# Softmax's causal zeroes written by GpSimd, with the units and the maxima in another order

## The chip, the cores and the metric

One Trainium2 chip, one of its cores. The metric is the device time of one launch in microseconds. Times of this kernel are the median of several launches; the profile is of one launch of its own.

## The reference, cut to what matters

The program is two transformer-like layers on x of 4 batches x 512 tokens x 128 features; each has a half-weighted feed-forward, attention, and another half-weighted feed-forward (first layer: dense; second: eight experts). The change touches the first layer's softmax attention alone, 16 heads of width 8:

```python
q, k, v = (_heads(q), _heads(k), _heads(x))
scores = jnp.einsum('bhqd,bhkd->bhqk', q, k) * scale
causal = jnp.tril(jnp.ones((t, t), dtype=bool))
scores = jnp.where(causal, scores, -jnp.inf)
y_ar = jnp.einsum('bhqk,bhkd->bhqd', jax.nn.softmax(scores, axis=-1), v)
e = v[:, :, 1:, :] - y_ar[:, :, :-1, :]
...
ma = jnp.einsum('bhqd,bhkd->bhqk', qa, ka)
ma = jnp.where(jnp.tril(jnp.ones((t - 1, t - 1), dtype=bool)), ma, 0.0)
y_ma = jnp.einsum('bhqk,bhkd->bhqd', ma, e)
```

So the softmax's answers y_ar are needed before the second, linear part (y_ma) of the same attention.

## The kernel before, in words

Each engine runs its own program, written out by hand: `nc.tensor` (PE), `nc.vector` (DVE), `nc.scalar` (ACT), `nc.gpsimd` (GpSimd, POOL in the profile) and `nc.sync` (SP, which issues the loads). They meet only in semaphores, and each engine's instructions, DMA issues included, run in the order of its program. `hold` (L310) is a wait that its engine makes before going on.

**Stages, sets, units, steps.** Attention of the first layer runs once for each batch b, as stage 0 to 3. In a stage the 16 heads are taken in four sets of four heads (hs, set 0 to 3). The 512 queries and 512 keys are cut in four tiles each; with causal masking 10 of the 16 pairs (key tile kt, query tile qt) remain. A pair for one set is one product of 128 keys x (4 heads x 128 queries), 512 columns. Five units i of two pairs each (`EXP_PAIRS`, L106, taken two by two) make a set, so a stage has 20 units, NX; a turn of the PE loop over u = 5 hs + i (L1636) is called a step here, step 0 to 4 of its set.

**Two passes.** The softmax subtracts a true row maximum. First pass, for batch b+1 while batch b is in its second: `max_scores` (L1541) makes a pair's scores with queries on partitions into one of two PSUM banks (`max_banks`), adds -1e30 above the diagonal by a second matmul (identity times `add_q_bf`), and DVE's `maxima` (L1100) reduces it to 128x4; 10 pairs a set, two in each step, the next on a bank only when its reduction is done. `max_of_tiles` and `max_turn` finish it, ACT writes the maxima as `mT`, and SP's `max_row` (L396) puts them as an extra row into the operand of the second pass. Stage 3 has no next batch and no first pass beside it.

Second pass: `scores` (L1561) makes unit u+2 in step u, into `pair[u % 2]`, as soon as the exponential of unit u has been read out of it. On a diagonal pair (kt = qt) a second matmul adds -1e30 to the forbidden places (`ident_bf` times `add_k_bf`, bf16, L1573). ACT's `attention` (L839) exponentiates both pairs of a unit at once, 128x1024 (L846), into the ten slots of `banks` (`sb_work` in the profile), which the next set overwrites; so it waits for the values products of the set before that read them (`LAST_OF_UNIT`). `answers` (L1576) multiplies a key tile's exponentials, all queries from the diagonal on (512, 384, 256 or 128 columns for kt 0 to 3), by the values, 4 heads in `accum[0]`, summed over kt. It runs in the step in which the last exponential of that tile is due: kt 0 in step 1, kt 1 in step 3, kt 2 and 3 in step 4. After a set ACT copies the sum out (`answers_out`, L832; it stands behind unit 0 of the next set), PE turns it in step 1 of the next set (`turn_answers`, L1588), DVE divides (`answers_divide`, L1139), and GpSimd makes the errors v - y (`errors`, L641). DVE's order of reductions and divisions is written in `at` (L1156), with the moments and the normalisation of batch b-1 (`moments`, `normalise`) between them; GpSimd supplies their inverse deviations (`rsqrt`) and later the bias (`add_bias`).

**SP.** In a stage before the last, SP goes set by set (L460): it holds until all ten maxima of the set are made (`smax_mm`), loads the maximum set two further (5 DMAs), holds for the scores of the set (`st_mm`), and loads the exponential set two further (5 DMAs) with its row of maxima (1 DMA). In stage 3 it holds for `st_mm` alone. Ahead of the sets stand `load_state` (the features of the linear part, 2 MB) and `load_values`. `scores` waits for `xset` at the first unit of a set (L1565).

```python
# SP, L460
for hs in range(NS):
    if b + 1 < B:
        next_max_set(b + 1, hs)
    hold(sp, s["st_mm"], NX * b + NG_X * (hs + 1))
    if hs + 2 < NS:
        load_exp_set(b, hs + 2)
        max_row(b, hs + 2)
```

After the four sets comes the linear part of the stage (`ma_scores`, `ma_answers`), which the change leaves as it is.

## Time and profile before

| | us |
|---|---|
| median of 3 runs | 645.68 (642.53 to 649.96) |
| the profiled execution, its own time | 643.67 |
| its span in the profile | 641.9 |
| PE busy | 521.5 (81%) |
| DVE busy | 359.4 (56%) |
| ACT busy | 197.0 (31%) |
| GpSimd busy | 189.0 (29%) |
| mean granted PE clock | 0.953 |

The span is from the first to the last instruction of the profiled execution. Busy time of an engine counts its instructions, not waits or the issue of DMAs. A matmul's end is modelled, and successive matmuls overlap: their pitch is the difference of their starts. The chain is the sequence of work that ended last, followed back from the end to whatever released each piece. All four attention stages together are the stretch from 115 to 343 us (115 to 173, 173 to 235, 235 to 296, 296 to 343).

### The profile page before, as it was taken

Reading aid. Unit: us, or ns where it says so; the run is one execution under the profiler, and the core shown is the slowest. Engines: PE = TensorE matmul, PEld = TensorE weight load, DVE = VectorE, ACT = ScalarE, POOL = GpSimd, SP = SyncE. Lnnn points to the kernel's source line nnn. Section 1 sums busy time; section 2 is a strip of 40 time slices with the busy share of each in tenths; the row PEclk is TensorE's granted clock in tenths of the full one; section 3 lists DMA queues with packets and bytes.
Section 4 is the critical chain, followed back from the end, with each engine's and each line's share of the span. In section 5 each row is a group of like instructions: output and inputs, shape, how many; then the busy total and the mean of one; then the engine's idle time right before and its main releaser. Section 6 shows DMA issues by size and latency. Waiting matters only on the chain.

```text
span 641.9 us, 10406 instructions
## 1 busy us (share of the span) xinstructions
PE 521.5 (81%) x3895; PEld 326.7 (51%) x3895; DVE 359.4 (56%) x942; ACT 197.0 (31%) x282; POOL 189.0 (29%) x228
## 2 busy tenths in 40 slices
PE   0788767999899989989877897894888878788893
PEld 0555333444544463445345773693345556663693
DVE  4753666466766767685044564132587888853131
ACT  0455331453154324424633450120223221110120
POOL 5676463010011102011110346654321212322163
PEclk9996798999999999999998997997998999988998
DMA  7317978732353244225269912323275455211320
GB/s 245 147 34 219 283 234 279 199 115 61 91 148 83 93 87 143 59 59 114 78 129 141 290 59 100 96 87 91 91 221 161 112 163 147 79 34 36 95 64 9
DMA packets 73666, 79.85 MB, mean 124 GB/s; under 512 B 10946, under 2 KB 50499, under 8 KB 73360
## 3 DMA queue, kind: packets, MB, share of 16 engines
q1 hardware_dynamic: 71056, 73.61, 41.4%
q0 software_dynamic: 2560, 5.58, 2.5%
q8 instruction: 31, 0.51, 0.3%
q14 instruction: 19, 0.16, 0.1%
HBM read 44.07 MB, written 35.72 MB: 124 GB/s over the span
## 4 chain that ended last, share of the span: by engine, by line
PE 49%; DVE 20%; issue 7%; DMA 6%; ACT 6%; POOL 5%; SPq 5%; POOLq 0%; DVEq 0%; ACTq 0%
PE ps_accum L1428 21%; PE ps_pair L1428 18%; PE ps_turn L1428 6%; DMA sb_ring<-sb_qs 3%; PE ps_turn L1436 2%; DVE sb_work L1178 2%; SPq L356 2%; POOL sb_rstd L569 2%; DVE sb_work L1323 2%; DVE sb_stats L1001 2%; DVE sb_mpart L1104 2%; SPq L350 1%; POOL xe_scr L589 1%; DMA sb_cols<-in_bias_cols 1%; PE ps_turn L1593 1%
## 5 line engine op out<-in xcount | busy, mean ns | idle before, releaser
L846 ACT ACTIVATE sb_work<-ps_pair 128x1024 f32<-128x1024 f32 x80 | 80.3, 1026 | 52.6 <-PE ps_pair L1428 51.8
L1104 DVE TENSOR_REDUCE sb_mpart<-ps_turn 128x4 f32<-128x512 f32 x80 | 55.0, 688 | 28.2 <-PE ps_turn L1428 28.1
L1428 PE MATMUL ps_pair<-sb_ring,sb_xsets 128*128 128x512 f32 x160 | 62.3, 465 | 6.7 <-ACT sb_work L846 3.5
L1104 DVE TENSOR_REDUCE sb_mpart<-ps_accum 128x4 f32<-128x512 f32 x80 | 55.0, 688 | 19.1 <-PE ps_accum L1428 18.3
L1428 PE MATMUL ps_pair<-sb_ident_bf,sb_ones_bf 128*128 128x512 bf16 x189 | 52.5, 437 | 12.1 <-DMA sb_x<-y_scr 7.8
L1428 PE MATMUL ps_accum<-sb_work,sb_v_aug 128*32 128x128 f32 (+3 forms) x768 | 53.9, 393 | 0.3 <-ACT sb_work L846 0.3
L1428 PE MATMUL ps_turn<-sb_ring,sb_m_sets 128*128 128x512 f32 x80 | 38.1, 477 | 9.4 <-DVE sb_mpart L1104 9.2
L567 POOL TENSOR_SCALAR sb_ve<-sb_mv 128x4 f32<-128x4 f32 x24 | 5.5, 228 | 133.5 <-DVE sb_mv L1004 126.9
L1428 PE MATMUL ps_accum<-sb_ring,sb_m_sets 128*128 128x512 f32 x80 | 40.6, 507 | 4.4 <-DVE sb_mpart L1104 3.8
L650 POOL TENSOR_TENSOR sb_e_pad<-sb_v_next,sb_y_ar 128x128 f32<-128x128 f32 x16 | 7.4, 460 | 122.8 <-DVE sb_y_ar L1148 122.8
L1428 PEld LDWEIGHTS ps_pair<-sb_ident_bf,sb_ones_bf 128*128 128x128 bf16 x189 | 20.4, 110 | 37.5 <-issue 13.2
L1323 DVE TENSOR_TENSOR sb_work<-ps_pair,sb_cst 128x1024 f32<-128x1024 f32 x32 | 37.5, 1214 | 2.2 <-PE ps_pair L1428 2.1
L1428 PEld LDWEIGHTS ps_pair<-sb_ring,sb_xsets 128*128 128x128 f32 x160 | 29.7, 192 | 17.7 <-issue 6.3
L1178 DVE TENSOR_TENSOR sb_work<-ps_pair,sb_cst 128x1024 f32<-128x1024 f32 x32 | 37.7, 1219 | 0.9
L1428 PE MATMUL ps_accum<-sb_mw,sb_work 128*128 128x128 f32 x256 | 31.3, 276 | 2.7 <-issue 2.7
L1272 DVE SCALAR_TENSOR_TENSOR sb_y_tmp<-ps_accum,sb_expert_rows 128x128 f32<-128x128 f32 x32 | 9.8, 347 | 42.0 <-PE ps_accum L1428 42.0
L1428 PE MATMUL ps_pair<-sb_y_tmp,sb_mw 128*128 128x256 f32 x128 | 30.7, 383 | 2.0 <-ACT sb_y_tmp L902 2.0
L1428 PE MATMUL ps_pair<-sb_xs,sb_w1r 128*128 128x512 f32 x64 | 23.6, 500 | 10.7 <-DVE sb_xs L1020 7.5
L589 POOL DMA_INDIRECT xe_scr<-sb_exit_rows,sb_slot_all x16 | 15.9, 995 | 53.4 <-DVE sb_slot_all L1085 49.8
L1428 PEld LDWEIGHTS ps_accum<-sb_mw,sb_work 128*128 128x128 f32 x256 | 30.0, 192 | 3.1 <-issue 3.0
L1428 PEld LDWEIGHTS ps_accum<-sb_work,sb_v_aug 128*32 128x32 f32 x768 | 18.8, 111 | 19.6 <-issue 13.4
L1428 PEld LDWEIGHTS ps_accum<-sb_ring,sb_m_sets 128*128 128x128 f32 x80 | 15.0, 188 | 25.9 <-DVE sb_mpart L1104 18.8
(251 smaller groups left out, 991.3 us busy)
## 6 DMA issues: line engine op xcount, KB each, us to landing
sb_expert_rows<-xe_scr SPq DMA_DIRECT2D x16, 258.0 KB, 2.8
sb_m_sets<-q_scr SPq DMA_DIRECT2D x16, 256.0 KB
sb_xsets<-k_scr SPq DMA_DIRECT2D x16, 256.0 KB
sb_ka_stk<-mk_scr SPq DMA_DIRECT2D x4, 1024.0 KB
xe_scr<-sb_cst SPq DMA_DIRECT2D x4, 1024.0 KB, 12.8
sb_mw<-in_mw SPq DMA_DIRECT2D x16, 256.0 KB, 6.1
sb_ka_stk<-mk_scr SPq DMA_DIRECT2D x8, 512.0 KB
q_scr<-sb_qs SPq DMA_DIRECT2D x12, 256.0 KB, 3.4
```

What stands on the lines that cost most here:

```text
L356: sp.dma_start(ring[VW * hl:VW * hl + 3 * HD, i, hl].bitcast(F32), head_rows(q_scr, b, HL * hs + hl, 3 * HD)).then_inc(done, 16)
L569: pool.tensor_tensor(rstd[i][:], ve[i][:], const("minus_half"), ALU.pow).then_inc(s["rstd"], 1)
L589: pool.indirect_dma_start(xe_scr[m], bass.IndirectOffsetOnAxis(ap=slot_all[:, i:i + 1], axis=0), rows_out[m][b][:, t, :], None).then_inc(s ...
L650: pool.tensor_tensor(dst, value, answer, ALU.subtract).then_inc(s["err_pad"], 1)
L846: act.activation(banks[:, 2 * i:2 * i + 2], pair[u % 2][:], ACT.Exp, scale=SCALE).then_inc(s["exp_done"], 1)
L1001: dve.bn_stats(stats[i][:, t, :], src[:, t, :]).then_inc(s["stats"], 1)
L1104: dve.tensor_reduce(mpart[:, m // NPAIR, m % NPAIR, :], max_banks[m % 2][:].rearrange("p (h k) -> p h k", h=HL), AX.X, ALU.max).then_inc(s ...
L1178: dve.tensor_tensor(work[:, n % 4].rearrange("p a (h q) -> p (a h) q", h=HL), pair[n % 2][:].rearrange("p a (h q) -> p (a h) q", h=HL), bc ...
L1272: last = dve.scalar_tensor_tensor(out=ye[n % 2][:, g, :], in0=accum[n % 2][:, g * D:(g + 1) * D], scalar=xg[:, n % 4, g, GATE:GATE + 1], i ...
L1323: dve.tensor_tensor(work[:, n % 4].rearrange("p a (h q) -> p (a h) q", h=HL), pair[n % 2][:].rearrange("p a (h q) -> p (a h) q", h=HL), bc ...
L1428: return pe.matmul(dst, lhsT, rhs, start=start, stop=stop, skip_group_check=True)
L1436: last = pe.transpose(tile(dst, t), src[:, t, 0:D], ident)
```

## The change

The mask matmul of the second pass goes: `scores` no longer adds -1e30 on diagonal pairs. The exponentials above the diagonal are written, whatever they are, and GpSimd then overwrites them with zero in place (`clear_late`, one `affine_select` for each unit that holds a diagonal). The units are regrouped (`EXP_UNITS`): (0,0) (0,1); (0,2) (0,3); (2,2) (3,3); (1,1) (2,3); (1,2) (1,3), so three selects a set, of 128x512, 128x1024 and 128x512. Values products run kt 0 in step 1, 3 in step 2, 2 in step 3, 1 in step 4, and each waits for GpSimd's `late_zero` as well. ACT copies the previous set's sum behind unit 1 instead of unit 0. The ten maxima of a set, two a step before, are spread 1, 3, 1, 2, 3 over its steps (`MAX_BESIDE`: before the values product, behind it, behind the turn), and DVE takes up nine of them before it normalises, not six. GpSimd's `rsqrt` and `add_bias` come behind the clears of set 0 and of unit 0 in set 1. The first pass keeps its mask matmuls, and SP's program is unchanged.

```diff
+EXP_UNITS = [((0, 0), (0, 1)), ((0, 2), (0, 3)), ((2, 2), (3, 3)), ((1, 1), (2, 3)), ((1, 2), (1, 3))]
+ANSWER_ORDER = [0, 2, 3, 1]
+READY_AT = [max(i for i, unit in enumerate(EXP_UNITS) for kt, qt in unit if kt == t) for t in range(NT)]
+LAST_OF_UNIT = [max(ANSWER_ORDER.index(kt) for kt, qt in unit) for unit in EXP_UNITS]
+CLEARED_UNITS = [i for i, unit in enumerate(EXP_UNITS) if any(kt == qt for kt, qt in unit)]
+MAX_BESIDE = [(1, 0, 0), (1, 1, 1), (1, 0, 0), (1, 0, 1), (1, 0, 2)]
...
+            def clear_late(b, hs, j):
+                i = CLEARED_UNITS[j]
+                pool.wait_ge(s["exp_done"], NX * b + NG_X * hs + i + 1)
+                weights = diagonal_slots(i).rearrange("p n (h q) -> p n h q", h=HL)
+                pool.affine_select(weights, weights, [[0, weights.shape[1]], [0, HL], [1, P]], ALU.is_ge, 0.0,
+                                   base=0, channel_multiplier=-1).then_inc(s["late_zero"], 1)
...
             def attention(b):
+                for j in range(len(CLEARED_UNITS)):
+                    clear_late(b, 0, j)
                 if b:
                     rsqrt(norm_first(B + b - 1), (b - 1) % 2)
-                    add_bias(norm_first(B + b - 1), b - 1, 0, s["ffn_base"])
-                for hs in range(NS - 1):
-                    errors(b, hs)
+                for hs in range(1, NS):
+                    clear_late(b, hs, 0)
+                    if b and hs == 1:
+                        add_bias(norm_first(B + b - 1), b - 1, 0, s["ffn_base"])
+                    clear_late(b, hs, 1)
+                    errors(b, hs - 1)
+                    clear_late(b, hs, 2)
...
-                    act.activation(banks[:, 2 * i:2 * i + 2], pair[u % 2][:], ACT.Exp, scale=SCALE).then_inc(s["exp_done"], 1)
-                    if hs and i == 0:
+                    act.activation(unit_slots(i), pair[u % 2][:], ACT.Exp, scale=SCALE).then_inc(s["exp_done"], 1)
+                    if hs and i == 1:
                         answers_out(b, hs - 1)
...
-                    at = [6] + [NPAIR * (hs + 1) + 3 for hs in range(NS - 1)] + [NM]
+                    at = [9] + [NPAIR * (hs + 1) + 3 for hs in range(NS - 1)] + [NM]
                     maxima(b + 1, 0, 4)
                     if b:
                         moments(norm_first(B + b - 1), x[b - 1], (b - 1) % 2)
-                    maxima(b + 1, 4, 6)
+                    maxima(b + 1, 4, 9)
...
-                    kt, qt = EXP_PAIRS[2 * i + a]
-                    last = mm(pair[u % 2][:, a, :], tile(x_sets[:, hs % 2], kt), ring[:, hs % 2, :, qt * P:(qt + 1) * P],
-                              stop=kt != qt)
-                    if kt == qt:
-                        last = mm(pair[u % 2][:, a, :], ident_bf[:], bc(add_k_bf[:], HL), start=False)
+                    kt, qt = EXP_UNITS[i][a]
+                    last = mm(pair[u % 2][:, a, :], tile(x_sets[:, hs % 2], kt), ring[:, hs % 2, :, qt * P:(qt + 1) * P])
...
-                pe.wait_ge(s["exp_done"], NX * b + NG_X * hs + (first + NT - kt - 1) // 2 + 1)
+                pe.wait_ge(s["exp_done"], NX * b + NG_X * hs + READY_AT[kt] + 1)
+                zeroed = next(j for j, i in enumerate(CLEARED_UNITS) if (kt, kt) in EXP_UNITS[i])
+                pe.wait_ge(s["late_zero"], len(CLEARED_UNITS) * (NS * b + hs) + zeroed + 1)
...
+                    m = NPAIR * hs + sum(map(sum, MAX_BESIDE[:i]))
+                    ends = [m + sum(MAX_BESIDE[i][:n]) for n in range(4)]
                     if ahead:
-                        max_scores(b + 1, 2 * u, 2 * u + 1)
-                    for kt in range(NT):
-                        if (DIAGONAL[kt] + NT - kt - 1) // 2 == i:
+                        max_scores(b + 1, ends[0], ends[1])
+                    for kt in ANSWER_ORDER:
+                        if READY_AT[kt] == i:
                             answers(b, hs, kt)
+                    if ahead:
+                        max_scores(b + 1, ends[1], ends[2])
                     if hs and i == 1:
                         turn_answers(b, hs - 1)
                     if ahead:
-                        max_scores(b + 1, 2 * u + 1, 2 * u + 2)
+                        max_scores(b + 1, ends[2], ends[3])
```

`slot_of`, `unit_slots` and `diagonal_slots` give the two slots of a unit, and those of its diagonals, in `banks`, whose layout is as before.

## Rows read from the trace of the kernel before

**Rows 1.** The page: chain by engine, and the exponential's group.
```profile
PE 49%; DVE 20%; issue 7%; DMA 6%; ACT 6%; POOL 5%; SPq 5%; POOLq 0%; DVEq 0%; ACTq 0%
...
L846 ACT ACTIVATE sb_work<-ps_pair 128x1024 f32<-128x1024 f32 x80 | 80.3, 1026 | 52.6 <-PE ps_pair L1428 51.8
```

**Rows 2.** Busy us by window, stages 1 and 3: PE, PEld, DVE, ACT, POOL, clock.
```profile
173.00:235.00 62.00, 56.57 (x432) 29.81 (x430) 42.72 (x77) 23.92 (x27) 6.63 (x12) 1.00 0.36 99
...
296.00:343.00 47.00, 40.53 (x371) 20.79 (x370) 15.88 (x33) 22.39 (x26) 6.04 (x11) 1.00 0.63 124
```

**Rows 3.** Chain in order of time: start us, us, what; stages 1 and 3.
```profile
192.51 2.67 DMA sb_ring<-sb_qs
...
197.62 0.46 PE ps_pair L1428 x2
...
199.76 0.69 PE ps_pair L1428 x3
...
307.66 3.17 DMA sb_ring<-sb_qs
```

**Rows 4.** SP's queue in order of time: start us, us; stages 0, 1, 3.
```profile
127.26 1.54 SPq L364 DMA_DIRECT2D sb_ring<-k_scr  x4
...
138.23 1.52 SPq L364 DMA_DIRECT2D sb_ring<-k_scr  x4
...
149.57 1.52 SPq L364 DMA_DIRECT2D sb_ring<-k_scr  x4
...
188.49 1.54 SPq L364 DMA_DIRECT2D sb_ring<-k_scr  x4
...
199.85 1.51 SPq L364 DMA_DIRECT2D sb_ring<-k_scr  x4
...
302.89 4.33 SPq L356 DMA_DIRECT2D sb_ring<-q_scr  x4
```

**Rows 5.** PE in order of time, stage 1: start us, us, [idle before].
```profile
186.44 0.50 PE L1428 MATMUL ps_turn<-sb_ring,sb_m_sets 128*128 128x512 f32 x1 [0.54 <-DVE sb_mpart L1104]
186.87 0.86 PE L1428 MATMUL ps_accum<-sb_work,sb_v_aug 128*32 128x256 f32 x16
187.66 0.50 PE L1428 MATMUL ps_accum<-sb_ring,sb_m_sets 128*128 128x512 f32 x1
...
190.99 1.07 PE L1428 MATMUL ps_accum<-sb_work,sb_v_aug 128*32 128x512 f32 x8
191.99 0.66 PE L1593 MATMUL ps_turn<-sb_cst,sb_y_tmp 128*128 128x128 f32 x4
192.40 0.48 PE L1428 MATMUL ps_accum<-sb_ring,sb_m_sets 128*128 128x512 f32 x1
...
194.05 0.51 PE L1428 MATMUL ps_accum<-sb_ring,sb_m_sets 128*128 128x512 f32 x1 [0.25 <-DVE sb_mpart L1104]
...
195.23 0.49 PE L1428 MATMUL ps_pair<-sb_ring,sb_xsets 128*128 128x512 f32 x1 [0.44 <-DMA sb_ring<-sb_qs]
```

**Rows 6.** PE in order of time, stage 3.
```profile
315.71 0.72 PE L1428 MATMUL ps_pair<-sb_ring,sb_xsets 128*128 128x512 f32 x2 [0.74 <-ACT sb_work L846]
...
323.50 0.72 PE L1428 MATMUL ps_pair<-sb_ring,sb_xsets 128*128 128x512 f32 x2 [0.74 <-ACT sb_work L846]
...
328.64 1.19 PE L1428 MATMUL ps_pair<-sb_qa_pad,sb_ka_stk 128*128 128x512 f32 x4
```

**Rows 7.** GpSimd's groups by line, 80 to 343 us: count, busy us, mean ns.
```profile
L650 POOL TENSOR_TENSOR sb_e_pad<-sb_v_next,sb_y_ar 128x128 f32<-128x128 f32 x16 | 7.4, 460 | 122.8 <-DVE sb_y_ar L1148 122.8
...
L691 POOL MEMSET sb_qa_pad<- 128x8192 f32 x1 | 6.9, 6929 | 0.0
L574 POOL TENSOR_TENSOR sb_x<-sb_x,sb_rows 128x512 f32<-128x512 f32 x4 | 5.1, 1272 | 3.7 <-DVE sb_kaf L1010 1.2 <-DVE sb_qf L1010 1.2 <-DVE sb_kf L1010 1.2
L569 POOL TENSOR_TENSOR sb_rstd<-sb_ve,sb_cst 128x4 f32<-128x4 f32 x3 | 3.1, 1037 | 0.3
...
L638 POOL COPY sb_v_aug<-sb_values 128x512 f32<-128x512 f32 x4 | 2.4, 610 | 21.1 <-DMA sb_values<-v_scr 11.1 <-PE ps_accum L1428 10.0
```

More of the change, by code:

```diff
@@ L96 @@
 ma_hi ma_lo mq_kept mk_kept state_in ka_t_mm ka_tok v_aug smax_mm smax_red max_t
-max_t_evac st_mm exp_done pv_mm y_evac y_t rcp y_norm err err_pad ma_mm ma_masked
+max_t_evac st_mm exp_done late_zero pv_mm y_evac y_t rcp y_norm err err_pad ma_mm ma_masked
 kv_mm kv_evac ym_mm yar_mm yar_evac y_sum proj_mm attn_base attn_x lg_mm lg_max lg_sub lg_exp
@@ L106 @@
 EXP_PAIRS = [(kt, qt) for kt in range(NT) for qt in range(kt, NT)]
-DIAGONAL = [EXP_PAIRS.index((t, t)) for t in range(NT)]
-LAST_OF_UNIT = [EXP_PAIRS[2 * i + 1][0] for i in range(NPAIR // 2)]
+EXP_UNITS = [((0, 0), (0, 1)), ((0, 2), (0, 3)), ((2, 2), (3, 3)), ((1, 1), (2, 3)), ((1, 2), (1, 3))]
[4 more added lines that the diff above has]
+MAX_BESIDE = [(1, 0, 0), (1, 1, 1), (1, 0, 0), (1, 0, 1), (1, 0, 2)]
 NM, NX, NG_X = NS * NPAIR, NS * NPAIR // 2, NPAIR // 2
@@ L121, in psum, with unit_slots, diagonal_slots @@
             return ctx.enter_context(nc.psum_tensor("ps_" + name, shape, F32))
+        slot_of = {pair: n for n, pair in enumerate(EXP_PAIRS)}
+        def unit_slots(i):
+            a, b = (slot_of[pair] for pair in EXP_UNITS[i])
+            return banks[:, a:b + 1:b - a]
+        def diagonal_slots(i):
+            a = [slot_of[pair] for pair in EXP_UNITS[i] if pair[0] == pair[1]]
+            return banks[:, a[0]:a[-1] + 1:max(a[-1] - a[0], 1)]
         s = {n: ctx.enter_context(nc.semaphore("s_" + n)) for n in SEMS}
@@ L1578, in answers @@
                 w = T - P * kt
-                first = EXP_PAIRS.index((kt, kt))
-                pe.wait_ge(s["exp_done"], NX * b + NG_X * hs + (first + NT - kt - 1) // 2 + 1)
+                first = slot_of[kt, kt]
+                pe.wait_ge(s["exp_done"], NX * b + NG_X * hs + READY_AT[kt] + 1)
+                zeroed = next(j for j, i in enumerate(CLEARED_UNITS) if (kt, kt) in EXP_UNITS[i])
+                pe.wait_ge(s["late_zero"], len(CLEARED_UNITS) * (NS * b + hs) + zeroed + 1)
                 if kt == 0 and hs >= 1:
@@ L1584, in answers @@
                     last = mm(accum[0][VW * hl:VW * hl + VW, kt * P:T], v_aug[:, kt, HL * hs + hl, :],
-                              banks[:, first:first + NT - kt, hl * P:(hl + 1) * P], start=kt == 0, stop=kt == NT - 1)
+                              banks[:, first:first + NT - kt, hl * P:(hl + 1) * P], start=kt == 0, stop=kt == ANSWER_ORDER[-1])
                 last.then_inc(s["pv_mm"], 1)
```

## The prediction

> **What bounds the kernel now.** I read the page's header and its chain by engine first [rows 1]: TensorE (PE) carries 49% of the chain that ended last, and SP's queue with the DMAs 11%. The table by stage [rows 2] has one row for each of the four attention stages, 228 us of the 641.9; stages 1 and 3 stand for them. In stage 1 (0 and 2 are alike), where PE also makes the next batch's maxima, PE is busy 56.57 of 62 us, 91%, at full granted clock, and GpSimd 6.63. Stage 3 has no maxima and PE is at 86%.
>
> Then the chain in order of time [rows 3]. In stage 1 it does not run along PE alone. The last maximum of set 0 ends about 188.4 and releases SP, which issues five loads of the next-but-one maximum set, five of the exponential set and one row of maxima [rows 4]. The row is issued at 192.51 and lands at 195.18, and only then does PE start set 2's first scores, in step 3 of set 1. PE waits 0.44 us there [rows 5]. So there is a loop: last maximum of a set, SP and DMA, steps 3 and 4 of the next set, its last maximum. It costs 195.23 - 188.4 = 6.8 plus 199.8 - 195.2 = 4.5, so 11.3 us; SP's own starts are 199.85 - 188.49 = 11.36 apart, in stage 0 10.97 and 11.34 [rows 4]. PE's work fits inside with a few tenths to spare. The loop holds sets 1 and 2 of stages 0 to 2, but not set 0 (its loads are in) nor set 3 (nothing is loaded for its steps 3 and 4).
>
> **The mask matmuls.** In the chain a group "x3" (two score products and a mask) takes 0.69 to 0.70 and "x2" 0.46 [rows 3], so a mask, like a product, is 0.23 us. The change drops 4 in a set, 64 in all: 14.7 us of PE work. What they are worth:
> Sets 1 and 2 of stages 0 to 2: steps 0 to 2 lose three masks (0.7), hand one maximum product and its mask to later steps (0.46), and take in key tile 3's values product (0.26, a third of the 0.79 from 186.87 to 187.66 [rows 5]). PE reaches step 3 about 0.9 us earlier and waits that much longer for the row. Steps 3 and 4 lose one mask, gain one maximum product and one of its masks (+0.23 net), and hold 640 instead of 768 columns of values products (-0.26): 4.5 us stays 4.5. SP's trigger stays the last maximum. Gain 0.
> Set 0: in stage 0 five masks lie on the path, 1.15 us; in stages 1 and 2 it starts at DVE's update of x, behind which lie four, 0.92. There PE also waits twice for reductions behind DVE's moments and normalisation, the second time 0.54 us [rows 5], together about one. The uneven spread leaves one maximum in step 2 beside the moments and moves the normalisation behind nine; I count 0.5 us of waits left, so 0.5 gained. Together 1.15 + 2 x 1.42 = 4.0.
> Set 3: three masks in steps 0 to 2 (0.69) and the 0.25 us wait for the reduction held behind the division [rows 5], whose successor now comes behind a score group: 0.94, less 0.3 that GpSimd's last clear is late (below), 0.64 x 3 = 1.9.
>
> **Stage 3.** Set 2's load is late for another reason: SP's four issues take 4.33 us, not the 1.5 of four others [rows 4], behind the features' loads, and the row lands at 310.83 [rows 3]. It hangs on those loads, begun as stage 2 ends, so earlier scores don't bring it forward. Nothing is gained up to 310.88; from there to the end of the last values products at 328.64 are 17.8 us. Before, each set closes a loop: last values product, ACT's copy of the sum, exponential of unit 1, 0.74 us wait of PE for it [rows 6], 323.50 - 315.71 = 7.8 us a set. The copy now comes after that exponential. By hand for one set, from the end of the second exponential: copy to 0.55 (half the exponential's columns), third exponential to 1.6, GpSimd clears the two diagonals by 3.3, key tile 3's product and the next scores to 4.1, the next exponential to 5.4, the one after it to 6.4. With scores at 310.88 the first such point is 313.6, the next 320.0, and the last product ends 6.1 later, at 326.1: 2.5 us gained.
>
> **What GpSimd's writes cost.** 48 selects come in, in each set two of 128x512 and one of 128x1024. The trace has none. Its nearest rows [rows 7]: a copy of 128x512, 0.61 us; a two-input add of the same size, 1.27; the memset of 8192 columns 6.93, 0.43 per 512. A select has one input and one output but must work out an index, so I take 0.9 us for 512 and 1.6 for 1024, between copy and add; bounds 0.6 and 2.0 for 512. Below the memset's 0.43 is excluded, since a select reads as well.
> At 0.9, from the start of step 1 with PE's pitches of 0.23 a product, 1.00 for key tile 0's values and 0.41 for the turn [rows 5]: step 1 lasts 2.8 us, and key tile 3's product comes at 3.5. The scores of its unit are made in step 0, its exponential (1.03 [rows 1]) ends about 0.8, the clear about 2.5: hidden. The last clear stands behind the errors of the set before (twice 0.46 [rows 7]), and these behind turn, reduction and division (3.55): it ends about 5.5. Set 3 wants it at 5.2, hence the 0.3; the middle sets want it after the wait for the load. Behind the waiting clears stand `rsqrt` and the bias (1.04 and 1.27 us [rows 7]): the deviations are needed after nine maxima, 8.3 us into the stage, and come at 7.3, one microsecond after the moments. The bias puts set 1's second clear to 13.1, wanted at 13.4. If that cover fails, it falls into the new wait for the load.
> The Trainium skill bears on this price (GPSIMD Engine Reference, Performance pitfalls for Q7 kernels): a loop that compares and selects runs at 2.03 cycles an element, 1.03 unrolled. At the page's 1.2 GHz that is an estimate of 0.44 to 0.87 us for 512, and the sum would be about 1 us better by it; no row here shows a select.
>
> **Sum.** 4.0 + 1.9 + 2.5 = 8.4 us off the profiled execution's 643.67, which is 635.3. The median of the runs is 645.68, 2.0 above it; the same gain from it gives 637.3. I take 636.0. A measurement of this kernel tells about 1% (6.4 us) from no change.
>
> **Rivals.**
> (a) All masks count, 14.7 us, and stage 3's shorter loop too: about 628. It needs SP's load to come sooner. Against it: the chain passes through that load, and SP's starts keep its spacing [rows 3, 4]. 0.10.
> (b) The select costs as much as the two-input add, 1.27 and 2.5 us. Then key tile 3's product waits 0.6 us in set 0 and the last clear 0.4 more in set 3, 3.0 over three stages; in stage 3 clears and errors stand in line, about 7.2 us a set and 328.4 for the end: 0.2 gained instead of 2.5. 8.4 - 3.0 - 2.3 = 3.1: about 641. For it: the index arithmetic; against it: only one operand is read. 0.20.
> (c) GpSimd becomes the bound, and the kernel slower: at 2.0 us for 512 a set needs 8 + 0.9 + 0.5 of handovers, 9.4 us in one queue. Stages 0 to 2 wait 2.0 in set 0, 0.3 in each middle set and 2.7 in set 3, 5.3 against 2.3 gained, so lose 3 each; stage 3 goes to 9.4 a set and loses about 3.5. Together 12: about 656. It decides from about 1.4 us for 512 columns. For it: GpSimd's spans are the least certain here; against it: copy and memset are a third of that. 0.17.
> A rule of the skill stands beside (c) (GPSIMD Engine Reference, Elementwise — side-by-side cycle accounting): data-dependent branching costs about 12 cycles an element. If the select did so, that is an estimate of 5 us for 512 columns, worse than (c). No row here shows such a loop.
>
> **How the numbers follow.** The forecast has 0.53. Its own range is 631 to 641, from set 0's waits, stage 3's loop, small handovers that I set at nothing, and the 2 us between profiled execution and median. Widened for (b) and the mild half of (c): 630 to 647; the faster part of (a) and the worse of (c) stay out. Faster by over 1% (below 639.2): (a) and nine tenths of the forecast, 0.58. Within 1%: (b) and the forecast's rest, 0.25. Slower: (c), 0.17.
>
> **What would show it.** The bf16 masks on `ps_pair` gone. PE's wait for `sb_ring<-sb_qs` in the middle sets grown from 0.44 to over 1 us, with SP's starts still 11.0 to 11.4 apart, and the last set 0.6 us shorter. In stage 3, 6.4 us a set from the third on. The select near 0.9 us. It would be wrong if the select is above 1.3, if PE waits for GpSimd ahead of `ps_accum`, or if the middle sets shorten.

## The result, and the profile after

The changed kernel takes 642.71 us (median of 12 runs, 638.78 to 648.01) beside 646.61 for the kernel before (12 runs): ratio 0.9938 [0.9911, 0.9966], some 4.0 us faster. The forecast was a time of 636.0, worked out from a gain of 8.4 on the profiled execution. The profiled execution after took 638.78, its span 637.0 against 641.9.

The page of the kernel after: the chain by engine, then groups (count, busy us, mean ns, idle before and its releaser). They answer to [rows 1, 7].
```profile
PE 44%; DVE 17%; SPq 10%; DMA 10%; issue 7%; POOL 5%; ACT 4%; POOLq 0%; DVEq 0%; ACTq 0%
...
L660 POOL TENSOR_SCALAR_AFFINE_SELECT sb_work<-sb_work 128x512 f32<-128x512 f32 (+1 forms) x48 | 37.9, 794 | 106.7 <-ACT sb_work L874 106.7
L1456 PE MATMUL ps_pair<-sb_ring,sb_xsets 128*128 128x512 f32 x160 | 57.3, 444 | 15.6 <-DMA sb_ring<-sb_qs 11.4
```
SP's queue and the DMAs carry 20% of the chain where they had 11%, and PE 44% where it had 49%. The score products now stand idle 11.4 us for the row of maxima.

GpSimd's groups after, 80 to 343 us, by form, beside [rows 7].
```profile
L660 POOL TENSOR_SCALAR_AFFINE_SELECT sb_work<-sb_work 128x512 f32<-128x512 f32 x32 | 20.6, 643 | 63.0 <-ACT sb_work L874 63.0
L660 POOL TENSOR_SCALAR_AFFINE_SELECT sb_work<-sb_work 128x1024 f32<-128x1024 f32 x16 | 17.5, 1097 | 43.7 <-ACT sb_work L874 43.7
```
A select takes 0.64 us for 512 columns and 1.10 for 1024, like the copy (0.61), not the 0.9 and 1.6 that I priced.

SP's queue after, in order of time, stages 0, 1 and 3 [rows 4]: start us, us.
```profile
116.37 8.48 SPq L400 DMA_DIRECT2D sb_values<-v_scr  x1
124.96 1.91 SPq L378 DMA_DIRECT2D sb_ring<-k_scr  x4
...
138.48 1.52 SPq L378 DMA_DIRECT2D sb_ring<-k_scr  x4
...
186.00 1.54 SPq L378 DMA_DIRECT2D sb_ring<-k_scr  x4
...
197.34 1.51 SPq L378 DMA_DIRECT2D sb_ring<-k_scr  x4
...
210.20 1.51 SPq L378 DMA_DIRECT2D sb_ring<-k_scr  x4
...
300.99 4.33 SPq L370 DMA_DIRECT2D sb_ring<-q_scr  x4
```
SP's start at 138.48 and its start at 210.20 come 13.52 and 12.86 us behind the one before; the interval between, 186.00 to 197.34, is 11.34, where the kernel before had 11.36. So the loop through SP is intact, but turns of it became longer. The first turn in stage 2 is a third one: 12.11 us, and 11.25 in the kernel before.

PE after, in order of time [rows 5, 6]: start us, us, [idle before].
```profile
132.31 0.72 PE L1456 MATMUL ps_pair<-sb_ring,sb_xsets 128*128 128x512 f32 x2 [2.90 <-DMA sb_ring<-sb_qs]
...
133.42 0.95 PE L1456 MATMUL ps_accum<-sb_work,sb_v_aug 128*32 128x256 f32 x8
...
144.91 0.73 PE L1456 MATMUL ps_pair<-sb_ring,sb_xsets 128*128 128x512 f32 x2 [1.34 <-DMA sb_ring<-sb_qs]
...
146.04 0.64 PE L1456 MATMUL ps_accum<-sb_work,sb_v_aug 128*32 128x256 f32 x8
...
192.69 0.73 PE L1456 MATMUL ps_pair<-sb_ring,sb_xsets 128*128 128x512 f32 x2 [0.96 <-DMA sb_ring<-sb_qs]
...
204.01 0.73 PE L1456 MATMUL ps_pair<-sb_ring,sb_xsets 128*128 128x512 f32 x2 [1.53 <-DMA sb_ring<-sb_qs]
...
309.12 0.74 PE L1456 MATMUL ps_pair<-sb_ring,sb_xsets 128*128 128x512 f32 x2 [1.65 <-POOL sb_work L660]
...
323.17 0.85 PE L1456 MATMUL ps_accum<-sb_work,sb_v_aug 128*32 128x384 f32 x8 [1.12 <-POOL sb_work L660]
```
The wait for the row grew from 0.44 to between 0.96 and 2.90 us (1.74 and 1.29 in stage 2). Behind the longest, the same eight values products take 0.95 us at 133.42 and 0.64 at 146.04. The table of windows of the kernel after says why (busy us of PE, PEld, DVE, ACT, POOL, then granted clock, DMA share, GB/s):
```profile
130.00:132.00 2.00, 0.00 (x0) 0.00 (x0) 0.18 (x1) 0.00 (x0) 0.41 (x1) 1.00 0.53 150
132.00:134.00 2.00, 1.69 (x12) 0.74 (x12) 0.47 (x1) 0.93 (x1) 0.00 (x0) 0.90 0.00 0
134.00:136.00 2.00, 2.00 (x8) 1.17 (x4) 0.91 (x2) 0.10 (x2) 0.64 (x1) 0.50 0.00 0
...
205.00:209.00 4.00, 4.00 (x21) 1.52 (x20) 2.08 (x3) 1.83 (x2) 0.64 (x1) 0.57 0.00 0
283.00:287.00 4.00, 3.60 (x38) 2.53 (x38) 2.86 (x5) 0.00 (x0) 0.00 (x0) 0.60 0.01 4
...
173.00:235.00 62.00, 54.48 (x415) 28.84 (x415) 43.06 (x78) 24.99 (x28) 16.01 (x25) 0.97 0.36 103
296.00:343.00 47.00, 38.10 (x358) 20.19 (x357) 16.87 (x34) 23.61 (x28) 15.35 (x23) 0.99 0.74 146
```
PE stood still from 129.4 to 132.3, went on at 2.4 GHz, and from about 133.6 to 137 had 1.2 GHz. The clock fell again at 205.3 (behind the 1.53 us wait) and at 283.8 (in the linear part), each time for 3.4 us. The profile of the kernel before shows no such stretch between 116 and 343 us. That is not a property of its program, though: the kernel before with one edit on SP (below) has four in its linear parts, and with one edit on ACT one in a middle set and one in a linear part. What a fall costs is read from two middle sets: from the landed row to SP's next start is 197.34 - 192.69 = 4.65 us at full clock, as forecast (4.5), and 210.20 - 204.01 = 6.19 with the fall: 1.5 us. In the profile of the SP edit just named, a linear part takes 7.22 us with a fall where it takes 5.75 without (161.13 to 168.35, and 162.22 to 167.97 in the kernel before): the same 1.5.

Stage lengths, from one stage's first output product (`ps_accum<-sb_wp,sb_w`) to the next one's (stage 0 from its first score, stage 3 to PE's first turn of a new x behind it):

| | stage 0 | 1 | 2 | 3 |
|---|---|---|---|---|
| before | 59.70 | 61.37 | 61.32 | 45.45 |
| after | 61.55 | 60.62 | 61.02 | 42.24 |
| after, a second profile (first run below) | 59.78 | 59.24 | 59.69 | 44.16 |

The second profile has no low clock inside stages 1 and 2. There, 2.13 and 1.63 us are gained, where I forecast 1.42 + 0.64 = 2.06. It began stage 0 at half clock (114 to 118 us) and has one fall inside the stages, in the linear part of stage 3. The linear part's start, and its first products with the errors, in the kernel before and in the second profile:
```profile
332.01 0.46 PE L1428 MATMUL ps_turn<-sb_v_next,sb_ka_tok 128*128 128x128 f32 x2 [1.74 <-POOL sb_v_next L651]
334.07 1.08 PE L1428 MATMUL ps_accum<-sb_work,sb_e_pad 128*32 128x128 f32 x32
```
```profile
324.65 0.46 PE L1456 MATMUL ps_turn<-sb_v_next,sb_ka_tok 128*128 128x128 f32 x2 [1.74 <-POOL sb_v_next L673]
327.19 1.94 PE L1456 MATMUL ps_accum<-sb_work,sb_e_pad 128*32 128x128 f32 x32
```
From that start to the end of stage 3 are 10.64 us before, 10.66 in the first profile and 11.91 in the second. Up to it, stage 3 takes 34.81, 31.58 and 32.25.

All four stages together gained 2.4 us in the first profile and 5.0 in the second. Outside of them, where the programs do the same, the first profile is 2.5 us shorter and the second 1.1 longer than the kernel before.

### The profile page after: what moved, and what is told of

It reads as the page before. It is cut to its first block, busy times and chain, and to the rows that moved or that the text cites. A ratio compares the mean times of both kernels' runs of the same rounds, so it can differ in the third digit from the quotient of the medians.

```text
span 637.0 us, 10379 instructions
## 1 busy us (share of the span) xinstructions
PE 509.4 (80%) x3831; PEld 322.7 (51%) x3831; DVE 359.7 (56%) x942; ACT 198.1 (31%) x282; POOL 226.3 (36%) x276
## 4 chain that ended last, share of the span: by engine, by line
PE 44%; DVE 17%; SPq 10%; DMA 10%; issue 7%; POOL 5%; ACT 4%; POOLq 0%; DVEq 0%; ACTq 0%
PE ps_accum L1456 20%; PE ps_pair L1456 14%; PE ps_turn L1456 6%; DMA sb_ring<-sb_qs 3%; DVE sb_work L1206 2%; SPq L378 2%; SPq L364 2%; PE ps_turn L1464 2%; DVE sb_work L1351 2%; SPq L370 2%; DMA sb_v_next<-v_scr 2%; DVE sb_mpart L1132 2%; DVE sb_stats L1029 1%; POOL sb_rstd L583 1%; SPq L400 1%
## 5 line engine op out<-in xcount | busy, mean ns | idle before, releaser
L660 POOL TENSOR_SCALAR_AFFINE_SELECT sb_work<-sb_work 128x512 f32<-128x512 f32 (+1 forms) x48 | 37.9, 794 | 106.7 <-ACT sb_work L874 106.7
L1456 PE MATMUL ps_pair<-sb_ring,sb_xsets 128*128 128x512 f32 x160 | 57.3, 444 | 15.6 <-DMA sb_ring<-sb_qs 11.4
L1456 PE MATMUL ps_pair<-sb_ident_bf,sb_ones_bf 128*128 128x512 bf16 x189 | 50.1, 421 | 12.3 <-DMA sb_x<-y_scr 8.0
L1456 PE MATMUL ps_accum<-sb_work,sb_v_aug 128*32 128x128 f32 (+3 forms) x768 | 58.1, 400 | 1.1 <-POOL sb_work L660 1.1
L1456 PE MATMUL ps_turn<-sb_ring,sb_m_sets 128*128 128x512 f32 x80 | 39.9, 499 | 8.9 <-DVE sb_mpart L1132 6.9
L1456 PEld LDWEIGHTS ps_pair<-sb_ring,sb_xsets 128*128 128x128 f32 x160 | 28.4, 194 | 26.6 <-DMA sb_ring<-sb_qs 13.3
L1456 PE MATMUL ps_accum<-sb_ring,sb_m_sets 128*128 128x512 f32 x80 | 36.8, 460 | 3.6 <-DVE sb_mpart L1132 3.1
L1456 PEld LDWEIGHTS ps_pair<-sb_ident_bf,sb_ones_bf 128*128 128x128 bf16 x189 | 19.8, 107 | 36.0 <-issue 10.5
L1456 PEld LDWEIGHTS ps_turn<-sb_ring,sb_m_sets 128*128 128x128 f32 x80 | 15.5, 194 | 43.4 <-DVE sb_mpart L1132 33.0
L1456 PEld LDWEIGHTS ps_accum<-sb_work,sb_v_aug 128*32 128x32 f32 x768 | 17.3, 111 | 24.1 <-issue 17.7
```

What stands on the lines that cost most here:

```text
L660: pool.affine_select(weights, weights, [[0, weights.shape[1]], [0, HL], [1, P]], ALU.is_ge, 0.0, base=0, channel_multiplier=-1).then_inc(s ...
L1456: return pe.matmul(dst, lhsT, rhs, start=start, stop=stop, skip_group_check=True)
```

## The experiments

All ratios are to the kernel before on the same chip, with 95% intervals.

**The changed kernel again.**

> The changed kernel as it is, for its time beside the others of this call and for a second profile. Theory (SP's loads hold the middle sets, and PE's longer wait for them now lets its clock fall): 0.994 of before, middle sets of stages 0 to 2 between 11.1 and 13.5 us by SP's starts, PE's granted clock at half for some 3.4 us once or twice behind such a wait. Rival (the slow stretches of the first profile were chance): the same time, but no stretch at the low clock inside stages 0 to 2 and all middle sets at 11.1 to 11.4.

Measured 0.9939 [0.9901, 0.9978], median 643.31: the result repeats. Its middle sets' waits for the row are 1.57, 1.44, 0.69, 2.00, 1.53 and 1.60 us, and its turns of the loop 11.1 to 11.9. The stretch at half clock that I expected behind such a wait did not come: a profile can be without one.

**SP's order turned round, with and without the change.** Both edits are the same, and move the next maximum set behind the exponential set:

```diff
-                    if b + 1 < B:
-                        next_max_set(b + 1, hs)
                     hold(sp, s["st_mm"], NX * b + NG_X * (hs + 1))
...
+                    if b + 1 < B:
+                        next_max_set(b + 1, hs)
```


> The changed kernel, with SP taking the exponential set and its row ahead of the maximum set, so that it waits for the scores of a set (step 2), not for its last maximum (step 4). Theory: PE's wait for the row of maxima in sets 2 and 3 is gone, the six middle sets take 9.7 to 10.0 us instead of 11.1 to 13.5, no low clock in stages 0 to 2: 8 to 11 us less than the changed kernel, about 0.98 of before. Rival (PE's own work or GpSimd's clears hold the middle sets): within 2 us of the changed kernel, the wait for DMA gone and as much waiting for GpSimd or DVE in its place.

> The kernel before with the same exchange on SP alone. Theory: its middle sets lose only the few tenths that PE waited, 11.1 to 10.4 at best, so 2 to 4 us, 0.995 of before; the difference to the exchange in the changed kernel is then what the masks are worth once the loads are out of the way, 6 to 9 us. Rival (the exchange brings the same in both kernels): 8 us or more here too.

Measured: on the changed kernel 0.9826 [0.9773, 0.9879], 634.11 us; on the kernel before 0.9953 [0.9917, 0.9989], 644.58. SP's queue in the first of them, stage 1:
```profile
187.38 1.77 SPq L370 DMA_DIRECT2D sb_ring<-q_scr  x4
...
189.58 0.59 SPq L412 DMA_DIRECT2D sb_ring<-sb_qs  x1
192.46 1.51 SPq L378 DMA_DIRECT2D sb_ring<-k_scr  x4
...
197.06 1.51 SPq L370 DMA_DIRECT2D sb_ring<-q_scr  x4
```
The row is issued behind the set's last scores, with no maximum awaited. PE's wait for it is gone, but for 1.12 us in the first middle set. From the start of one set's exponential loads to the next, middle sets take 9.66 to 9.72 us with the change (10.08 the first one) and 10.64 to 10.68 without: 0.97 us, the four masks of a set (0.92). So the loop was what hid them. The two ratios differ by 0.0127, 8 us, give or take 4 by their intervals; the medians differ by 10.5. In the profiles, stages 1 and 2 differ by 5.2 us each, 1.5 of it a fall of the clock in the linear part of the one that keeps the masks. So with the loads out of the way the same change is worth some 3.7 us a stage, about twice what it gained alone in stages 1 and 2 of the second profile (2.13 and 1.63).

**What a wait does to PE's clock.** Five matmuls without a purpose ahead of the waits of sets 2 and 3:

```diff
+                if i == 0:
+                    if hs >= 2 and b + 1 < B:
+                        stay_awake(5, pair[u % 2][:, 0])
+                    pe.wait_ge(s[f"xset{hs % 2}"], 96 * (2 * b + hs // 2 + 1))
```


> The changed kernel, with five idle matmuls of 512 columns (about 1.2 us) ahead of PE's wait for the loads of sets 2 and 3 in stages 0 to 2; their bank is overwritten by the scores. Theory: the wait is filled, the clock stays at full, and the sets that took 12.9 and 13.5 us come down by about 1.6 us each; 1 to 4 us less than the changed kernel, never more. Rival (the long sets come from late loads alone): the same time within 1 us, the sets still 12 to 13.5.

Measured 0.9916 [0.9881, 0.9952], 641.31 us; the interval overlaps that of the changed kernel. The clock is clearer than the time: averaged over the runs, the mean granted clock was 0.9528 before, 0.947 with the change, 0.9537 here. But it was 0.9466 in the changed kernel with SP's order turned, where these waits are gone too; its profile has two falls, both in stage 3. The second version has such matmuls in stage 3's set 2 too, and four of them ahead of the linear part of every stage:

```diff
+                    if hs == 2 or (hs == 3 and b + 1 < B):
+                        stay_awake(5, pair[u % 2][:, 0])
...
+                pe.wait_ge(s["attn_x"], b)
+                stay_awake(4, accum[1])
                 pe.wait_ge(s["ka_tok"], b + 1)
```

> The changed kernel, its waits for loads in stages 0 to 3 and its waits for GpSimd ahead of the linear part all filled with idle matmuls, five and four of 512 columns; nothing else is moved. Theory (the clock takes back 2 to 3 us of the change's gain): mean granted clock at or above that of before, time 0.987 to 0.990 of before. Rival (late loads alone take the gain back, and the clock is chance): mean clock as in the changed kernel, 0.992 to 0.996.

Measured 0.9879 [0.9823, 0.9935], 638.80 us, clock 0.9545. PE in this run, set 2 of stage 0:
```profile
131.90 1.25 PE L1456 MATMUL ps_pair<-sb_ident_bf,sb_ones_bf 128*128 128x512 bf16 x5
133.33 0.72 PE L1456 MATMUL ps_pair<-sb_ring,sb_xsets 128*128 128x512 f32 x2 [0.17 <-DMA sb_ring<-sb_qs]
```
There is no fall in it from 120 to 336 us. The middle sets stay at 11.1 to 11.5 by SP's starts, so only the clock was mended. The second half of this edit, alone in the kernel before:

> The kernel before with the four idle matmuls ahead of the linear part alone. Theory (the falls of the clock behind waits are what the changed kernel added, the one before has few inside these stages): mean clock up by at most 0.002, time 0.996 to 1.000 of before. Rival (the fill is worth the same in every kernel, 2 us or more): 0.995 or less.

Measured 0.9983 [0.9948, 1.0019], 646.21 us: no gain that can be told there. The kernel before has no clock to win back (0.9567 against 0.9551 beside it).

**The masks alone, put back into the changed kernel.**

```diff
+                    if kt == qt:
+                        last = mm(pair[u % 2][:, a, :], ident_bf[:], bc(add_k_bf[:], HL), start=False)
```


> The changed kernel with the 64 mask matmuls put back beside the clears, which then find zeroes. Theory: the middle sets stay at 11.0 to 11.4 us and PE's wait for the loads shrinks by 0.7; the first and last sets of stages 0 to 2 get 0.9 and 0.7 us longer, stage 3 little; the clock stays at full more often: 1 to 4 us more than the changed kernel, 0.996 to 1.000 of before. Rival (each mask counts 0.23 us): 14 us more, about 1.015 of before.

Measured 0.9993 [0.9954, 1.0031], 647.34 us. 14.7 us of PE work are worth 0.0055, some 3.6 us. With them the waits for the row shrink to 0.55 to 1.08 us, and the middle sets stay at 11.16 to 11.55, 68.6 us for all six, as many as in the second profile of the changed kernel (68.7): here the masks lie inside the wait.

**ACT's copy behind unit 1, alone in the kernel before.**

```diff
-                    if hs and i == 0:
+                    if hs and i == 1:
```


> The kernel before, with ACT's copy of the sum behind unit 1 instead of unit 0 and nothing else. Theory: stage 3's sets go from 7.8 to about 7.0 us where no load is late, 1 to 2 us in all, 0.998 of before; stages 0 to 2, held by loads, stay. Rival (the masks make stage 3's gain): sets of 7.8 us still.

Measured 0.9948 [0.9908, 0.9988], 645.21 us. In stage 3 the sets take 7.86 and 6.78 us, from 8.36 and 7.79. Its linear part starts here:
```profile
329.51 0.46 PE L1428 MATMUL ps_turn<-sb_v_next,sb_ka_tok 128*128 128x128 f32 x2 [1.74 <-POOL sb_v_next L651]
332.05 1.94 PE L1428 MATMUL ps_accum<-sb_work,sb_e_pad 128*32 128x128 f32 x32
```
That is 32.29 us behind the stage's start, where the kernel before needs 34.81: the copy's place alone gains 2.5 us. The whole stage, 44.18, shows only 1.3 of it, because the clock falls in the linear part, as the 1.94 us for 32 products show. The rival falls; and what the changed kernel gained in stage 3 up to its linear part, 3.2 and 2.6, is nearly all the copy's. The ratio can't be told from the changed kernel's own 0.9938, and is more than its profile shows (stages 0 and 1 are 59.79 and 61.17, stage 2 has a wait of 1.40 for the row and a fall of the clock). Nor does it add up with the masks put back (0.9993, with the copy in its new place): at 0.4% on either side, single parts of 2 or 3 us can't be summed.

**The selects made twice.**

```diff
+                pool.affine_select(weights, weights, [[0, weights.shape[1]], [0, HL], [1, P]], ALU.is_ge, 0.0,
+                                   base=0, channel_multiplier=-1).then_inc(s["late_once"], 1)
+                pool.wait_ge(s["late_once"], len(CLEARED_UNITS) * (NS * b + hs) + j + 1)
```


> The changed kernel with each select made twice, the second waiting for the first, so 1.3 and 2.2 us in place of 0.64 and 1.10: the price of my rival (b). Theory (the selects are hidden in stages 0 to 2 while the loads hold the middle sets, and in line in stage 3): 2 to 5 us more than the changed kernel, most of it in stage 3 and the last sets, so about 0.998 to 1.001 of before. Rival (GpSimd has so much room that even the double is hidden): within 1 us of the changed kernel.

Each select is followed by itself, 1.3 and 2.2 us in all. Measured 1.0008 [0.9963, 1.0054], 648.58 us. PE's waits in this run, 116 to 343 us (total us, times, longest):
```profile
PE ps_pair L1459 <- DMA sb_ring<-sb_qs: 9.8, 6, 3.0
PE ps_accum L1459 <- POOL sb_work L663: 6.1, 5, 1.8
```
All five waits for GpSimd stand in stage 3, which takes 47.15 us, 1.4 of them a fall in its linear part; stages 0 to 2 hide even the doubled select. In all it took back the change's gain.

**Maxima spread evenly (two a step) in the changed kernel.**

```diff
-MAX_BESIDE = [(1, 0, 0), (1, 1, 1), (1, 0, 0), (1, 0, 1), (1, 0, 2)]
+MAX_BESIDE = [(1, 0, 1)] * 5
...
-                    maxima(b + 1, 4, 9)
+                    maxima(b + 1, 4, 6)
```
and 6 for 9 in `at`.

> The changed kernel with two maxima in each step and the normalisation behind six, as before. Theory: set 0 of stages 1 and 2 gets back its waits for reductions, about 1 us each, and the middle sets stay at 11.1 to 11.4 since the loads hold them; 1 to 2.5 us more than the changed kernel, 0.995 to 0.998 of before. Rival (the spread does nothing): within 0.5 us, waits for reductions as in the changed kernel.

Measured 0.9952 [0.9917, 0.9987], 644.75 us, not told apart from 0.9938. Its profile shows what the spread is for: PE waits 3.5 us in all for reductions on `ps_turn`, up to 1.1 us each, and none with the uneven spread. From the start of stages 1 and 2 to set 0's last maximum, as SP's start shows it, are 14.1 us here, 14.0 in the kernel before and 11.9 in the changed one, and 12.8 with the masks put back: without the spread the missing masks gain nothing there. But the middle sets did not stay, as I had expected. Their turns take 10.60 to 11.33 us, 65.5 for the six, where the kernel before has 67.2 and the second profile of the changed kernel 68.7. So the uneven spread wins 4.4 us in set 0 of stages 1 and 2 and gives 3.2 back in the middle sets.

**Stage 3 and GpSimd's queue.** The clear of unit 3 ahead of the errors of the set before:

```diff
-                    errors(b, hs - 1)
                     clear_late(b, hs, 2)
+                    errors(b, hs - 1)
```


> The changed kernel with the third clear of a set ahead of the errors of the set before on GpSimd. Theory (in stage 3 PE's wait for GpSimd, 1.65 us before 309.1, comes from that clear standing behind errors that wait for the features' loads): that wait is gone in set 1, and the 1.1 us wait in set 3 too; 1 to 2 us less in stage 3, as far as the load of set 2 is in by then, nothing in stages 0 to 2. Rival (the selects themselves are late): the waits for GpSimd stay within 0.3 us.

Measured 0.9947 [0.9904, 0.999], 644.36 us. PE's waits for GpSimd's clears are gone, as expected, and the load is late instead; stage 3 up to its linear part takes 32.45 us, so nothing is gained:
```profile
308.16 0.86 PE L1456 MATMUL ps_pair<-sb_ring,sb_xsets 128*128 128x512 f32 x2 [1.88 <-DMA sb_ring<-sb_qs]
```

**The values' load behind set 0's loads.**

```diff
-                if b + 1 < B:
-                    load_values(b + 1)
...
                         max_row(b, hs + 2)
+                    if hs == 0 and b + 1 < B:
+                        load_values(b + 1)
```

> The changed kernel with the next batch's values loaded behind set 0's loads and nothing else. Theory (part of the new wait in set 1 is SP still held in the issue of the values' load, and the DMA queue behind it): set 1's wait for its load in stage 0 falls from 1.5 to 2.9 us to about 1, in stage 2 from 1.5 to about 1, the later sets' stay; 1 to 2 us less than the changed kernel. Rival (the loads' own length sets the waits): all waits as in the changed kernel, same time.

Measured 0.9882 [0.9833, 0.9931], 641.11 us. The waits for the row did not fall as expected: 1.35 and 1.49 us in stage 0, 1.70 and 1.94 in stage 2. Stage 1 is 58.75 and stage 3 is 41.82; stage 2 is 61.74, with a fall of the clock behind the 1.94, and stage 0 is 59.52, with PE's clock at half from 114 to 117. Whether stage 0 gains by this edit stays open.

**All loads in order of need.** The values' load as above, SP's order turned round, in stage 3 the features' loads behind set 0's, and the clears ahead of the errors:

```diff
-                load_state(b)
                 if b + 1 < B:
-                    load_values(b + 1)
+                    load_state(b)
...
                     if b + 1 < B:
                         next_max_set(b + 1, hs)
+                        if hs == 0:
+                            load_values(b + 1)
+                    elif hs == 0:
+                        load_state(b)
```


> The changed kernel with SP's exponential set ahead of its maximum set (as in the earlier run), the next values loaded behind set 0's loads, stage 3's features behind its set 0 loads, and on GpSimd all three clears of a set ahead of the errors (stage 3's first errors later still). Theory: stage 0's set 1 no longer waits about 1 us for its load, and stage 3's sets 0 and 1 wait neither for the load (1.5 to 2.9 us) nor for GpSimd behind the features; 2 to 4 us less than with the exchange on SP alone, 0.976 to 0.980 of before. Rival (stage 3's first sets are held by PE and ACT): as with the exchange alone, 0.983.

Measured 0.9863 [0.9817, 0.9909], 640.11 us: stage 3 went wrong, 49.49 us. Its SP queue, and then PE:
```profile
298.19 8.53 SPq L370 DMA_DIRECT2D sb_ring<-q_scr  x4
```
```profile
310.32 1.22 PE L1463 MATMUL ps_pair<-sb_ring,sb_xsets 128*128 128x512 f32 x2 [6.39 <-DMA sb_ring<-sb_qs]
```
The features only moved from ahead of set 2's load to ahead of set 3's, where PE has nothing left to do. With the four matmuls ahead of the linear part added:

> The kernel with the loads in order of need and four idle matmuls of 512 columns (0.9 us) in PE's wait of 1.1 to 1.7 us for GpSimd's last errors, ahead of the linear part. Theory (the clock falls behind waits of about a microsecond, each fall costs up to 1.7 us): fewer falls in the linear parts, mean granted clock 0.005 higher, 1 to 4 us less than without them. Rival (those falls come from elsewhere): same clock within 0.002, same time within 1 us.

Measured 0.9785 [0.9743, 0.9827], 634.42 us, mean granted clock over the runs 0.9478 for 0.9405: stages 56.03, 56.43 and 56.50, and still 47.81 in stage 3. Then the features behind set 1's loads:

```diff
-                    elif hs == 0:
+                    elif hs == 1:
                         load_state(b)
```

> As the kernel with loads in order of need and filled waits, with stage 3's features behind the loads for set 3 instead of those for set 2. Theory (in stage 3 the new wait of 6.2 us before set 3 was the row of maxima behind 2 MB of features): that wait is gone, stage 3 takes 40 to 42 us instead of 47.8, 6 us less in all, about 0.969 of before. Rival (the features then come too late for GpSimd's errors ahead of the linear part): a wait of several microseconds for GpSimd there, and 0.975 to 0.98.

Measured 0.9858 [0.9808, 0.9908], 639.17 us, stage 3 at 51.39. From the chain of this run, and PE:
```profile
302.12 11.97 DMA sb_v_next<-v_scr
```
```profile
316.60 1.94 PE L1463 MATMUL ps_accum<-sb_work,sb_v_aug 128*32 128x512 f32 x8 [9.57 <-POOL sb_work L663]
```
My own mistake: the first clear of set 3 stands behind the errors in GpSimd's queue, these wait for the features, and the features now landed at 314.

**The parts that helped, put together,** with the features at the front of every stage again (the 0.9785 kernel less one edit):

```diff
-                if b + 1 < B:
-                    load_state(b)
+                load_state(b)
...
-                    elif hs == 0:
-                        load_state(b)
```

> The changed kernel with everything that helped put together: SP takes the exponential set and its row ahead of the next maximum set, the next values behind set 0's loads (stages 0 to 2), the features at the front of every stage as in the change, GpSimd clears a set's three places ahead of the errors (in stage 3 the errors of sets 0 and 1 behind set 2's clears), four idle matmuls ahead of the linear part. My theory (the change gains its masks once the loads are out of the way): no wait for sb_ring<-sb_qs in stages 0 to 2, middle sets 9.7 us, stages 56.0, 56.4, 56.5, and stage 3 about 41 to 44 because neither the 2 MB features stand ahead of set 2's load late, nor the clears behind them; together 16 to 19 us below the kernel before, ratio 0.970 to 0.975. Rival (the loads of a stage only change places: features at the front delay set 2's row whatever SP's order): stage 3 stays at 45 to 47 us and the ratio at 0.978 to 0.985.

Measured 0.9726 [0.9677, 0.9776], 629.09 us, by the ratio 17.8 us below the kernel before. Windows of stages 1 and 3, then PE's one wait for a load behind stage 0's start:
```profile
173.00:235.00 62.00, 57.32 (x441) 30.82 (x441) 44.92 (x81) 27.59 (x31) 17.18 (x26) 1.00 0.44 114
296.00:343.00 47.00, 38.46 (x355) 23.50 (x354) 17.13 (x36) 19.93 (x25) 12.02 (x20) 0.96 0.78 112
```
```profile
300.72 0.72 PE L1460 MATMUL ps_pair<-sb_ring,sb_xsets 128*128 128x512 f32 x2 [2.15 <-DMA sb_ring<-sb_qs]
```
Stages 1 and 2 are 56.45 and 56.43, as expected, stage 3 is 41.90. Stage 0 is 58.0, not 56.0: its first six microseconds ran at half clock. This version beats both kernels.

## Why the prediction was wrong

The forecast of 8.4 us was double what came; the direction held. The range 630 to 647 held too, but by luck: 642.71 lies outside the forecast's own 631 to 641, and the range had been widened for a select that costs more, which it does not.

Here is the sum, term by term, in us gained against the profile of the kernel before (each rounded by itself). Set 0 goes up to SP's start behind its last maximum, the middle sets are the two turns of the loop behind it, set 3 ends with its own last maximum; stage 3 stands up to its linear part.

| | forecast | first profile | second profile |
|---|---|---|---|
| set 0, stages 0 to 2 | 4.0 | 4.2 | 3.9 |
| middle sets, stages 0 to 2 | 0 | -4.8 | -1.5 |
| set 3, stages 0 to 2 | 1.9 | 1.2 | 1.2 |
| stage 3 | 2.5 | 3.2 | 2.6 |
| the rest, linear parts | none | -1.4 | -1.3 |
| together | 8.4 | 2.4 | 5.0 |

**The middle sets: the step that failed.** The loop was read right: the masks' removal did not shorten it, and turning SP's order round took the middle sets to 9.7. But "reaches step 3 about 0.9 us earlier and waits that much longer ... Gain 0" put a price of nothing on the longer wait and on what stands inside it. The six sets became 4.8 us longer in one profile and 1.5 in the other. Of the 4.8, 3.0 are two falls of the granted clock to half, behind waits of 1.5 and 2.9 us, at 1.5 us a fall. What is left, 1.8, and the 1.5 of the second profile, is no clock: in some turns SP's issue or the row's load takes longer than before. In the first turn of stage 2, PE goes on 3.43 us behind the row's issue (250.63 to 254.06), in stage 1 2.66. Why the row is later there is not shown. The run with the even spread shows that the loop had something to win: its six sets take 65.5 us, 67.2 before. The uneven spread gave that away.

**The linear parts: not in the sum.** In each of the two profiles one fall in a linear part costs 1.3 to 1.4 us. The wait ahead of it, for GpSimd, is as long in the kernel before, and with SP's order turned the kernel before has such falls in all four stages. So this loss is not shown to be the change's.

**What the clock costs over all runs** is less sure. The first profile has two falls in middle sets, the second none. Over all profiles here, 7 of 34 waits of 0.9 to 3.1 us for the row in these sets have a fall behind them; in the profiles where these waits are shorter, gone or filled there is one wait of that length, and no fall. So it is well supported that the falls there come from the waits; which wait brings one is open. The mean granted clock fell from 0.953 to 0.947, and single runs of one kernel are 3 to 4 us longer for each 0.01, so an estimate of the whole loss is 2 us. Most of the time at half clock lies outside of the attention stages, though (62 us in all in the profile before, 55 and 62 in those after), so the mean does not say where it was lost. Filling waits raised the mean by 0.007 in two pairs of kernels (0.947 to 0.9537, and 0.9405 to 0.9478); with all of them filled the time went from 0.9938 to 0.9879, with intervals that overlap.

**Set 0: the sum right, the parts not.** From the first score behind DVE's update of x to set 0's last maximum, 11.8 us became 9.7: 2.1 gained in each of stages 1 and 2 where I had 1.42. In stage 0 I had 1.15, and the gain is 0. In the first profile PE did reach the tenth maximum 0.6 us sooner (11.0 us behind its first score, from 11.6), but SP was still in the issue of the values' load, 8.48 us long, until 124.85. Its first maximum set starts 12.41 us behind the first score, before it was 12.45. I had moved work past SP's queue and not asked when that queue is free. In the second profile SP was free at 125.21, and the tenth maximum came only at 125.63, 11.9 us behind the first score, since the stage began at half clock. That the two errors cancel is luck.

**Set 3: a third short.** Last maximum of set 2 to that of set 3: 9.71 us before, 9.30 after, 0.4 for 0.64.

**Stage 3: the sum right, for the copy's sake.** The shorter loop is there: 6.21 us a set, forecast 6.4. Up to the linear part the stage gained 3.2 us in one profile and 2.6 in the other, forecast 2.5. But the kernel before with the copy moved and nothing else gained 2.5 there: little or nothing is left for the masks. What varies is the start. Either the row is late by up to 2.3 us, or the clear of unit 3 ends late: it stands behind the errors, which in set 1 wait for the features' load, and PE waits 1.65 us at 309.12. I had put the clear behind the errors, but not the errors behind the load. One of my signs of being wrong came with it: PE also waits for GpSimd ahead of `ps_accum`, 1.12 us at 323.17.

**The select: cheaper than priced.** 0.64 and 1.10 us for 0.9 and 1.6; it is hidden in stages 0 to 2 even doubled, so rivals (b) and (c) fall. The doubled one (1.3 us) is (b)'s price, and took back 0.007, 4.5 us, which is nearer to (b)'s 5 than its places: I had put 3.0 of them into stages 0 to 2, where no wait for GpSimd is found. The Trainium skill (GPSIMD Engine Reference, Performance pitfalls for Q7 kernels), from which the prediction drew an estimate of 0.44 to 0.87 us for a compare and select of 512, agrees with the 0.64 measured. Its 12 cycles an element for data-dependent branching (same page, Elementwise — side-by-side cycle accounting), an estimate of 5 us for 512, are not what this instruction costs.

**Rival (a)**, all masks count, needed SP's load to come sooner. It did not by itself; with SP's order turned it came to 634, and with everything together to 629.

So in the two profiles the terms that I counted on brought 8.6 and 7.7 us, and the middle sets and linear parts took back 6.2 and 2.7. The ratio says about 4 over all runs, between the 2.4 and the 5.0.

## What to carry to other kernels

Work removed from the busiest engine is worth nothing inside a loop that closes over a load; look for what releases the load, and turn that queue's order first. If the engine then waits longer, ask what the wait does to its clock, and whether what it waits for comes as soon as before: a gain of 0 can be a loss. Compare the forecast with the profile term by term, since errors cancel in the sum. Where an edit bundles several moves, run each alone: here the copy's new place was nearly all of stage 3's gain. And for every instruction moved, ask what the instructions ahead of it in its own queue wait for, the DMA issues of SP included.

## What was not expected of the hardware

- PE's granted clock can fall to half (1.2 GHz) behind a single wait in a stretch in which PE is otherwise over 90% busy, and the fall comes 1.3 to 1.4 us after PE has gone on (204.01 to 205.3; 132.31 to 133.6). The shortest wait for the row with a fall behind it is 1.40 us (before 254.75 in the run with the copy alone moved). The waits of 1.34 us before 144.91 and 1.74 before 254.06 in the first profile did not bring it, nor did that of 2.00 us in the second: whether a wait of this length costs 1.5 us or nothing differs from case to case.
- One DMA issue on SP's queue can take 8.48 us (the values' load at 116.37, behind the features' 2 MB), where the same one took 0.39 us behind set 0's loads (130.81 in the run that moved it). What stands behind it in SP's program waits as well.
- An affine select on GpSimd costs about as much as a copy of the same size: 0.64 us for 128x512, where the copy takes 0.61, and 1.10 for 128x1024.
